# Second cross attention of a four-layer kernel: maxima transposed by an identity matmul, thirteen probability buffers, other PSUM banks

## The reference, cut to what matters

```python
qn = layernorm(x, ln_q_g, ln_q_b)            # x: 8 x 256 x 256
q = qn @ Wq * scale                          # 16 heads of 64
k, v = jnp.split(media @ Wkv, 2, axis=-1)    # media: 8 x 1601 x 128
sim = jnp.einsum('bhid,bhjd->bhij', q, k)
sim = jnp.where(media_mask[:, None, None, :], sim, neg_inf)
attn = jax.nn.softmax(sim, axis=-1)
out = jnp.einsum('bhij,bhjd->bhid', attn, v)
```

## Time and profile before

| | |
|---|---|
| median of three runs | 3692.28 us (3692.16 to 3707.71) |
| profiled execution | 3699.85 us |
| its span, first to last instruction | 3698.1 us |
| mean granted clock of TensorE | 0.967 |
| busy, of the span | PE 3345.8 us (90%), DVE 2020.4 (55%), ACT 1811.6 (49%), POOL 1590.0 (43%) |
| this stage's steady part | about 1650 to 3110 us |

### The profile page before, as it was taken

How to read it: one execution, slowest core, us unless ns; L and a number is a source line. 1 busy time by engine, 2 the same in 40 slices (tenths; PEclk the granted TensorE clock), 3 DMA queues, 4 the chain that set the end, 5 groups by cost and what they waited for, 6 DMA issues and landing times. The chain is left out here.

```text
span 3698.1 us, 73901 instructions
## 1 busy us (share of the span) xinstructions
PE 3345.8 (90%) x25048; PEld 2358.0 (64%) x25048; DVE 2020.4 (55%) x3324; ACT 1811.6 (49%) x3374; POOL 1590.0 (43%) x1421
## 2 busy tenths in 40 slices
PE   7798799898999799979998999899999998999997
PEld 5556544444444588856666666666666666888886
DVE  4475577787777355435555555555555553114454
ACT  2254377676767433435555555555555553333333
POOL 3213022221221021117777777777777776004554
PEclk9899799999999899979999999999999999999998
DMA  4784200000000232120000000000001002310200
GB/s 120 165 136 112 74 7 17 18 17 17 17 30 12 97 114 100 76 92 13 26 18 14 31 16 28 11 31 14 29 13 56 16 13 76 113 51 32 96 7 12
DMA packets 74750, 179.34 MB, mean 48 GB/s; under 512 B 14720, under 2 KB 44928, under 8 KB 68480
## 3 DMA queue, kind: packets, MB, share of 16 engines
q1 hardware_dynamic: 70240, 161.81, 14.4%
q0 software_dynamic: 4128, 12.60, 1.3%
HBM read 115.09 MB, written 59.26 MB: 47 GB/s over the span
## 5 line engine op out<-in xcount | busy, mean ns | idle before, releaser
L1654 POOL TENSOR_TENSOR cross_acc<-cross_acc,cross_probs 128x512 f32<-128x512 f32 (+1 forms) x704 | 919.9, 1307 | 252.5 <-ACT cross_probs L1718 203.1
L1718 ACT ACTIVATE cross_probs<-cross_s,cross_bias 128x512 f32<-128x512 f32 (+1 forms) x832 | 508.7, 685 | 642.6 <-PE cross_s L1924 527.2
L1807 DVE TENSOR_REDUCE cross_partmax<-cross_r 128x1 f32<-128x400 f32 (+1 forms) x1024 | 541.3, 570 | 395.9 <-PE cross_r L1894 379.4
L1256 DVE TENSOR_REDUCE cross_partmax<-cross_m 128x2 f32<-128x800 f32 (+1 forms) x512 | 496.9, 991 | 183.9 <-PE cross_m L1359 182.9
L1167 ACT ACTIVATE cross_probs<-cross_s 128x512 f32<-128x512 f32 (+1 forms) x832 | 453.3, 595 | 149.2 <-PE cross_s L1379 148.7
L1937 PE MATMUL cross_av<-cross_probs,cross_v 128*64 128x256 f32 (+1 forms) x3328 | 426.8, 395 | 0.0
L1937 PEld LDWEIGHTS cross_av<-cross_probs,cross_v 128*64 128x64 f32 (+1 forms) x3328 | 220.1, 138 | 164.1 <-issue 40.2
L1106 POOL TENSOR_TENSOR cross_diag<-c_ident,cross_negmax 128x256 fp32r<-128x256 f32 x128 | 75.8, 613 | 496.4 <-DVE cross_negmax L1264 496.4
L1796 DVE TENSOR_TENSOR cross_k_lo<-cross_r,cross_k_hi 128x400 fp32r<-128x400 f32 (+1 forms) x256 | 146.2, 572 | 255.7 <-ACT cross_k_hi L1695 255.7
L1390 PE MATMUL cross_av<-cross_probs,cross_v 128*32 128x256 f32 (+1 forms) x3328 | 268.0, 394 | 10.0 <-ACT cross_probs L1167 8.5
L1894 PE MATMUL cross_r<-cross_k_hi,cross_q_hi 64*128 64x400 f32 (+1 forms) x1024 | 222.8, 405 | 42.4 <-ACT cross_ln_sum L1730 33.7
(11 more groups left out here) (307 smaller groups left out, 6507.9 us busy)
## 6 DMA issues: line engine op xcount, KB each, us to landing
d_masked_ctx<-tail_ctx_split SPq DMA_DIRECT2D x8, 1602.0 KB, 5.3
d_self_qk<-selfproj_qk_split POOLq DMA_DIRECT2D x32, 256.0 KB, 5.5
self_qs<-d_self_qk SPq DMA_DIRECT2D x64, 128.0 KB, 8.2
self_ks<-d_self_qk SPq DMA_DIRECT2D x64, 128.0 KB, 8.6
d_cross<-tail_pr SPq DMA_DIRECT2D x8, 1024.0 KB, 4.6
cross_qp<-d_cross SPq DMA_DIRECT2D x64, 128.0 KB, 2.3
d_cross<-cross_out SPq DMA_DIRECT2D x64, 128.0 KB, 1.8
tail_attn<-d_cross SPq DMA_DIRECT2D x8, 1024.0 KB, 5.4
```

The lines of the kernel that those rows point to most:

```text
L1256: nc.vector.tensor_reduce(partmax[:, :, jt // 2, jt % 2, i:i + 1], m_pair(sets[q], w), AX.X, ALU.max).then_inc(maxed, 1)
L1654: nc.gpsimd.tensor_tensor(acc[0:w, g % 2], left, probs[0:w, slot % NPB], ALU.add).then_inc(added, 1)
L1718: nc.scalar.activation(probs[0:w, (g * KT + t) % NPB], src_, ACT.Exp, scale=XHD ** -0.5, bias=bias[0:w, p, t:t + 1]).then_inc(probs_ready, 1)
L1807: nc.vector.tensor_reduce(partmax[:, m, i:i + 1], r_ps[banks[q]][:, 0:KCH[i][1]], AX.X, ALU.max).then_inc(maxed, 1)
```

## The change

Three things, all in `cross_attention_1`. (1) `diag` and its VectorE instruction go. The reduction writes the negated maxima straight into columns 0 and 64 of a zeroed 128 x 128 matrix for each half t of the queries, and the shift multiplies these two matrices (as weights, fp32) by the identity: the result is their transpose, with the maxima of head h in row 64h and zeros elsewhere. (2) Every tile of probabilities has a buffer of its own, nine in `probs` and four in the space of the fp32 weights `w`, which is used up once w_lo is built. (3) Sums go to bank 2, the first value tile of a unit to bank 0, and the maxima of phase 0 use 2, 1, 0, 2; the waits in `max_item` follow.

```diff
-        partmax, negmax = ph.sb("partmax", [P, 4, NC]), ph.sb("negmax", [P, 4])
-        diag = ph.sb("diag", [P, 2, S], F32R)
+        partmax, negmax = ph.sb("partmax", [P, 4, NC]), ph.sb("negmax", [P, 2, P])
-        NPB = 8
-        probs, acc = ph.sb("probs", [P, NPB, 2, S]), ph.sb("acc", [P, 2, 2, S])
+        NPB = KT
+        probs, acc = ph.sb("probs", [P, NPB - 4, 2, S]), ph.sb("acc", [P, 2, 2, S])
+        more_probs = w[:].rearrange("p (k h s) -> p k h s", k=4, h=2)
...
-        EARLY = 2 * PRIME
+        EARLY = 4 * PRIME
...
-        K_BANK, V_BANK, SHIFT_BANK, SUM_BANK = (1, 1, 1, 1), 2, 0, 0
-        MAX_BANK = (0, 1, 2, 0) * 4
+        K_BANK, V_BANK, SHIFT_BANK, SUM_BANK = (1, 1, 1, 1), (0, 2, 2, 2), 0, 2
+        MAX_BANK = (2, 1, 0, 2) + (0, 1, 2, 0) * 3
...
+        def prob(t):
+
+            return probs[:, t] if t < NPB - 4 else more_probs[:, t - NPB + 4]
...
-                    slot = g * KT + t
-                    left = probs[:, (slot - 1) % NPB] if t == 1 else acc[0:w, g % 2]
-                    nc.gpsimd.tensor_tensor(acc[0:w, g % 2], left, probs[0:w, slot % NPB], ALU.add).then_inc(added, 1)
+                    left = prob(0) if t == 1 else acc[0:w, g % 2]
+                    nc.gpsimd.tensor_tensor(acc[0:w, g % 2], left, prob(t)[0:w], ALU.add).then_inc(added, 1)
...
                         act.wait_ge(bias_ready, b + 1)
+                        act.wait_ge(w_lo_ready, 2)
...
                     act.wait_ge(probs_used, number - NPB + 1 + EARLY)
-                    act.wait_ge(added, n * (KT - 1) + (t - NPB + 1 if t < NPB else max(t - NPB, 1)) + EARLY)
+                    act.wait_ge(added, (n - 1) * (KT - 1) + max(t, 1) + EARLY)
...
-                    nc.scalar.activation(probs[0:w, (g * KT + t) % NPB], src_, ACT.Exp,
+                    nc.scalar.activation(prob(t)[0:w], src_, ACT.Exp,
                                          scale=XHD ** -0.5, bias=bias[0:w, p, t:t + 1]).then_inc(probs_ready, 1)
...
+                nc.vector.memset(negmax[:], 0.0).then_inc(zeroed, 1)
+                dve.wait_ge(zeroed, 1)
...
-                def diagonals(u):
+                def negative_maxima(u):
                     b, p, g, n = u
                     dve.wait_ge(maxed, (n + 1) * NM + PRIME)
-                    dve.wait_ge(diag_ready, n + PRIME)
-                    nc.vector.tensor_reduce(negmax[:], partmax[:], AX.X, ALU.max, negate=True).then_inc(negmax_ready, 1)
-                    dve.wait_ge(negmax_ready, n + 1 + PRIME)
                     dve.wait_ge(shift_ready, n + PRIME)
-                    nc.vector.tensor_tensor(diag[:].rearrange("p j (t s) -> p (j t) s", t=2),
-                                            c["ident"][:].unsqueeze(1).to_broadcast([P, 4, P]),
-                                            negmax[:].unsqueeze(2).to_broadcast([P, 4, P]), ALU.mult).then_inc(diag_ready, 1)
+                    nc.vector.tensor_reduce(negmax[:].rearrange("p t (h x) -> p h t x", h=2)[:, :, :, 0],
+                                            partmax[:].rearrange("p (h t) i -> p h t i", h=2), AX.X, ALU.max,
+                                            negate=True).then_inc(negmax_ready, 1)
...
-                    pe.wait_ge(diag_ready, n + 1 + PRIME)
-                    for h in range(2):
-                        last = nc.tensor.matmul(r_ps[SHIFT_BANK][:, 0:S], c["sel_r"][:, 2 * h], diag[:, h],
-                                                start=(h == 0), stop=(h == 1))
+                    pe.wait_ge(negmax_ready, n + 1 + PRIME)
+                    for t in range(2):
+                        last = nc.tensor.matmul(r_ps[SHIFT_BANK][:, t * P:(t + 1) * P], negmax[:, t], c["ident"][:],
+                                                start=True, stop=True)
                     last.then_inc(shift_ready, 1)
...
@@ -1984,11 +1987,18 @@
 
                     n, after, k = nxt[3], following(nxt, NP), q // 4
                     if q == 0:
+                        pe.wait_ge(k_ready, (n + 1) * NC + PRIME)
+                        if before and value_tile(before, NQ - 1):
+                            pe.wait_ge(v_ready, value_made(before, NQ - 1) + PRIME)
+                    elif q == 2:
                         pe.wait_ge(shifted, n + PRIME)
-                        pe.wait_ge(k_ready, (n + 1) * NC + PRIME)
-                    elif q == 2 and before and value_tile(before, NQ - 1):
-                        pe.wait_ge(v_ready, value_made(before, NQ - 1) + PRIME)
+                    elif q == 3:
+                        pe.wait_ge(maxed, n * NM + 1 + PRIME)
+                    elif q == 4 and value_tile(u, 0):
+                        pe.wait_ge(v_ready, value_made(u, 0) + PRIME)
                     elif q == 4:
+                        pe.wait_ge(maxed, n * NM + 3 + PRIME)
+                    elif q == 6:
                         pe.wait_ge(ln_ready, n - 1 + PRIME)
                         pe.wait_ge(maxed, n * NM + 4 + PRIME)
                     elif q % 4 == 1 and k and after:
...
-                        v_tile(*made, r_ps[V_BANK])
+                        v_tile(*made, r_ps[V_BANK[k]])
```

More of the change, by code:

```diff
@@ L1557, in cross_attention_1 @@
             ph.sem(n) for n in ("kp_ready", "kh_ready", "k_ready", "vp_ready", "v_ready", "qh_ready", "q_ready"))
-        max_ready, maxed, negmax_ready, diag_ready, shift_ready, shifted = (
-            ph.sem(n) for n in ("max_ready", "maxed", "negmax_ready", "diag_ready", "shift_ready", "shifted"))
+        max_ready, maxed, negmax_ready, zeroed, shift_ready, shifted = (
+            ph.sem(n) for n in ("max_ready", "maxed", "negmax_ready", "zeroed", "shift_ready", "shifted"))
         s_ready, probs_ready, probs_used, added, av_copied, sum_ready, rsum_ready, out_ready = (
@@ L1636, in _ @@
             def _(pool):
-                prime(pool, added, added, q_ready, out_ready)
+                prime(pool, added, added, added, added, q_ready, out_ready)
                 def queries_low(u):
@@ L1832, in ahead @@
                         maxima(u, q, MAX_BANK_AHEAD)
-                    diagonals(u)
+                    negative_maxima(u)
                     copy_shift(u)
@@ L1846, in step @@
                         if k == NQ - 1:
-                            diagonals(nxt)
+                            negative_maxima(nxt)
                         if after:
@@ L1857, in _ @@
             def _(pe):
-                prime(pe, kp_ready, vp_ready, max_ready, shift_ready, s_ready, probs_used, probs_used, sum_ready)
+                prime(pe, kp_ready, vp_ready, max_ready, shift_ready, s_ready, probs_used, probs_used, probs_used, probs_used, sum_ready)
                 def k_chunk(u, i, banks=K_BANK):
@@ L1937, in values @@
                             last = nc.tensor.matmul(av_ps[h * XHD:(h + 1) * XHD, 0:S], v[0:w, g // 4, t, d0:d0 + XHD],
-                                                    probs[0:w, (g * KT + t) % NPB, h], start=(t == 0), stop=(t == KT - 1))
+                                                    prob(t)[0:w, h], start=(t == 0), stop=(t == KT - 1))
                         last.then_inc(probs_used, 1)
```

2 lines of the change are left out of this document (1 added, 1 removed).

## The result

| | before | after |
|---|---|---|
| median of four runs of each, in turn on one chip | 3696.2 us (3692.16 to 3707.71) | 3601.93 us (3598.07 to 3608.09) |
| profiled execution (span) | 3699.85 (3698.1) | 3598.37 (3596.6) |
| mean granted clock | 0.967 | 0.972 |
| first to last shift of the stage | 1644.19 to 3096.14: 1451.95 | 1634.73 to 2992.96: 1358.23 |

The change takes 94 us: the ratio is 0.9742, with a 95% interval of 0.9712 to 0.9771. The forecast was 3580 us and a gain of 112; the time lies inside the range. The stage itself gives 93.7 us, nearly all of it. (Ahead of its first shift the profiled execution has another 9.5 us, mostly less time at the low clock in code that the change doesn't touch; that part varies from run to run.)

The account below looks back on a forecast made before the run. TensorE, busy 1336 of 1460 us, was taken as the bound, leaving 124 us of standing and low-clock time. 80 (diagonal) - 16 (shift) + 35 (banks) - 3 (end) + 16 (clock) = 112 us, so 3580 us, range 3552 to 3620.

Parts of the forecast that it names:

- Diagonal: Before the shift matmuls, TensorE no longer waits for VectorE's diagonal: 1.37 us an ordinary unit, 0.97 every fourth, 80 us.
- Transposition: At the shift, two fp32 matmuls run as four instructions and cost 0.25 us more a unit, 16 us in 63 units.
- The row: Profile row of L1346, fp32 128x128 against 128 columns, 0.123 us each, taken as the price of each shift instruction.
- The lower bound of the forecast: For the shift's added cost: -0.1 us a unit if half the columns were half the time.
- Banks: At q = 4 behind the sums, TensorE no longer waits for ScalarE's logarithm: 0.55 us a unit, 35 us; above, 0.66.
- One of the signs named against the forecast: In the profile after, maxima waiting for a value tile would show the forecast wrong; no size given.
- Buffers: Thirteen probability buffers: ScalarE no longer waits for the sum eight tiles back (107.2 us); costed at nothing.
- Clock: In the steady part, all ten falls to half clock behind the shift's gap go, 1.55 us each: 16 us.
- Rival (a): The low clock stays, falls hanging on sparse values and sums, about ten times: 3596 us; chance 0.08.
- The end: In the last two units GpSimd does not keep up, so the gain of 1.7 us each is mostly lost: -3 us.
- Both should be over by then: At q = 0 and q = 2, the moved waits for old value tile and copied shift cost nothing.
- Rival (b): VectorE's shift copy, behind ScalarE's high key part, becomes the scores' new wait: 0.5 us a unit, 3612 us; chance 0.10.

Follow-up runs that it names:

- e4: The changed kernel with VectorE's high part of the queries made directly behind the negated maxima, ahead of the last low key part; 3574.04 us, 0.9686 of before.
- e6: The changed kernel with the two transposing matmuls of the shift made twice, eight instructions in place of four; 3594.01 us, 0.973 of before.
- e5: e4 with negated maxima and identity in fp32r, so each transposing matmul is one instruction and not two; 3560.58 us, 0.9633 of before.
- e2: The kernel before with the new banks alone, keeping the diagonal and eight buffers; 3657.2 us, 0.9904 of before.
- e3: The kernel before with the thirteen buffers alone, keeping the diagonal and old banks; 3692.7 us, 1.0008 of before.
- e8: The changed kernel with eight buffers in place of thirteen, so transposition and banks together; 3594.1 us, 0.972 of before.
- e1: The kernel before with the transposition alone, keeping eight buffers and the old banks; 3624.96 us, 0.9817 of before.

## Why the prediction was right or wrong

**Diagonal, 1.37 us in an ordinary unit: right.** Its arithmetic closes on the units of e4: 22.80 - 1.37 (diagonal) + 0.21 (shift) - 0.66 (banks) = 20.98 us, and e4 has 20.93 and 20.98. With e4's 0.32 us put back it is 21.30, and the change has 21.31 and 21.40.

**Transposition, 0.25 us: nearly right**, 0.21. The row was the right one to go by: 0.123 us there, 0.112 for each added instruction in e6, and not the 81 ns of the Trainium skill (TensorE: Matmul & The Clock Gate, Back-to-back issue gap). The lower bound of the forecast, -0.1 us, does not follow from its own terms: half of 0.12 us for each of four instructions makes 0.24, as much as before. Two instructions, in e5, hold TensorE for 0.37 us and so save 0.06 against the old pair.

**Banks, 0.55 us: a little small**, 0.66 by e2, which was the upper bound given. The place that was read, between the sums and q = 4, gave 0.56. One of the signs named against the forecast did appear, if only for 3.6 us in the stage: maxima that wait for a value tile (L1707), 0.26 us each.

**Buffers, nothing: right** (e3, e8). But the reason was half wrong. "ScalarE no longer waits for the sum" was taken from an inferred releaser; it never did in that place.

**Clock, ten falls, 16 us: right, and shown** by e1 (all gone in the units) and e2 (more of them). Rival (a) falls with it. That two falls stand behind the closings of the loop was not in the sum.

**The end, -3 us: right in size, but not where it was put.** The last three times from shift to shift still gained 1.43, 1.30 and 1.73 us. Behind the last shift 1.2 us are lost: the last sum starts 23.01 us behind it and before 21.85; 0.7 of that is the last wait, 5.77 in place of 5.07 us. And the 12 units ahead of the last three gained only 1.22 us each, since their gap was 1.28 us and not 1.51. The earlier trace rows showed that, and the term of the diagonal took 1.37 us for all.

**The step that failed**, though the time lies inside the range, is under the banks: "Both should be over by then (rival b says how nearly)", about what q = 0 and q = 2 wait for. It followed the shift copy alone, and q = 0 needs another thing that VectorE makes behind that copy: the high part of the queries. The margin was to be had from the kernel before, whose timeline has, between the copy and the q = 0 of the earlier trace rows:

```profile
2322.71 0.35 DVE L1790 CAST cross_q_hi<-cross_qp 128x256 fp32r<-128x256 f32 x1
```

It ends at 2323.06, 0.64 us ahead of q = 0 at 2323.70, and the forecast moved q = 0 forward by 0.97 - 0.25 = 0.72 us in such a unit and by 1.12 in an ordinary one (where the margin is 0.64 us too, but VectorE's chain can start sooner). Rival (b) had the right mechanism, a chain from ScalarE through VectorE that becomes the new wait, and 0.5 us a unit for it; it named the copy as its last link, and the scores as the victim, each one place off. Its price by e4 is 0.32 us a unit, 20 us of the whole. The waits of the change hang on one chain: exponentials, high part of the keys (ScalarE), low part, shift copy, high part of the queries (VectorE), q = 0.

**The second miss**: the closings of the loop. Those two units went from 26.12 and 26.04 us to 28.70 and 29.24, up by 5.8 us and not down by 3.1.

Over the stage the accounts are: 46 units at -1.41 us, 12 at -1.22 and the last three at -1.49 give -84.0 (forecast -96 + 3 = -93); the two at the closings +5.8 (forecast -3); ten falls of 1.55 us -15.5 (as forecast). The sum is -93.7 against -112. The 9 us that the 61 units lack are not one miss: the wait for the queries took about 19 us there by e4, and some 9 of them came back by luck, because banks and shift turned out better by 0.11 and 0.04 us a unit. The 22 us between 3580 and 3601.93 are these 18 and 4 us by which the median of before lay higher in the runs beside the change.

## What to carry to other kernels

When a wait is taken away, list everything that the instruction behind it needs, and for each the engine's whole queue up to it, with its end time in the trace before: the one with the least margin is the next wait, and what stands last in a slack engine's queue is often it. An inferred releaser of an instruction with several waits is a hint; look whether the data it reads were there. And an idle time just long enough to let the clock fall costs more than itself: here gaps of 1.5 us cost another 1.55 us in ten of 63 units.

## What was not expected of the hardware

- Idle time of "issue" where the loop closes depends on what TensorE's stream consists of, from 1.8 to 3.9 us, and repeats in each run of one program. It ends 1.7 to 2.4 us behind a packet of the instruction queue q8, and is long where two of these overlap; why they do is open.
- The same gap of 1.51 us led to ten falls of the clock in units of 22.80 us, to 13 in e3 with the same units, and to 18 in units of 22.14 (e2), each in one execution. The gap alone doesn't decide whether one comes. In the units whose gap at the shift was 1.30 us or less, the first and those at the closings apart, none came in any trace.
- Matmuls with the identity, eight in a row with nearly only zeros as weights, brought no fall of the clock (e6). By the Trainium skill (TensorE: Matmul & The Clock Gate, Part 4: PE-mode transpose) a transpose in PE's own mode doesn't count as busy. Whether a plain matmul with the identity is such, e6 doesn't show: even if its eight counted as standing, the gap would be 0.15 + 1.09 = 1.24 us, and gaps of 1.27 to 1.30 us brought no fall before either.
- VectorE's conversion of the queries took 0.35 us before, 0.55 us in the change and 0.88 us in e4, ahead of the low key part; why is open. It cost nothing there, since VectorE would have been idle.
